# Row fetches of a graph-and-attention kernel divided over two more queues, and the cell's output kept in PSUM

## The reference, cut to what matters

```python
x = x + gnn(layernorm(x), edge_index)      # x is 6250 x 256
x = x + slice_attention(layernorm(x))      # 8 heads, 64 slices

agg = segment_sum(x[src], dst)             # 106,250 edges, sorted by dst
h = relu(agg @ W_rel + b_rel + x @ W_root) # 512 wide
i, f, g, o = split(h @ W_ih.T + b_ih + b_hh)
c = sigmoid(i) * tanh(g)
h_lstm = sigmoid(o) * tanh(c)
y = h_lstm @ W_fc + b_fc
```

## Time and profile before

| what | value |
|---|---|
| three runs | 1239.16, 1241.82, 1243.43 us; median 1241.82 |
| the profiled execution | 1240.34 us, of which 1238.5 us is the span from first to last instruction |
| PE busy | 1116.1 us (90%), granted clock 0.994 |
| DVE, POOL, ACT busy | 831.8 (67%), 805.3 (65%), 627.2 us (51%) |
| 22 turns from 184.60 to 1084.19 us | 899.59 us, 40.89 us each |

### The profile page before, as it was taken

One profiled execution on the slowest core, in us unless ns is written; L12 is line 12 of the kernel. 1 busy time (PEld: TensorE's weight loads), 2 busy tenths in 40 slices (PEclk: granted clock), 3 DMA queues, 4 the chain that ended last, 5 costly groups with the idle time before them and its releaser, 6 DMA issues. The chain is left out here.

```text
span 1238.5 us, 30254 instructions
## 1 busy us (share of the span) xinstructions
PE 1116.1 (90%) x9821; PEld 967.1 (78%) x9821; DVE 831.8 (67%) x2560; ACT 627.2 (51%) x1257; POOL 805.3 (65%) x856
## 2 busy tenths in 40 slices
PE   1077799999999999999999999999999999999998
PEld 0046688878888888788888787888888878897798
DVE  7885476667666766676677756775767566746665
ACT  5872444554456454545554545455545454555332
POOL 5877777777777777777777777777777777400000
PEclk9998999999999999999999999999999999999999
DMA  8674444444454445444544444444444454313498
GB/s 313 225 268 119 125 130 136 147 142 136 129 148 142 141 124 150 140 140 123 150 149 138 121 148 150 137 121 150 147 136 122 150 149 137 97 44 116 129 336 290
DMA packets 92966, 188.74 MB, mean 152 GB/s; under 512 B 20914, under 2 KB 55591, under 8 KB 92821
## 3 DMA queue, kind: packets, MB, share of 16 engines
q0 software_dynamic: 39168, 107.01, 30.0%
q1 hardware_dynamic: 42794, 59.89, 14.8%
q10 hardware_dynamic: 10859, 20.05, 4.5%
HBM read 154.87 MB, written 32.00 MB: 151 GB/s over the span
## 5 line engine op out<-in xcount | busy, mean ns | idle before, releaser
L700 POOL DMA_INDIRECT ring<-table,sidx x798 | 763.5, 957 | 247.5 <-issue 242.7
L419 PE MATMUL ps<-h_h,wih_h 128*128 128x250 f32 x1200 | 338.8, 282 | 0.0
L420 PE MATMUL ps<-h_l,wih_h 128*128 128x250 f32 x1200 | 336.5, 280 | 0.0
L421 PE MATMUL ps<-h_h,wih_l 128*128 128x250 f32 x1200 | 336.5, 280 | 0.0
L419 PEld LDWEIGHTS ps<-h_h,wih_h 128*128 128x128 f32 x1200 | 230.1, 192 | 2.0 <-issue 0.8
L420 PEld LDWEIGHTS ps<-h_l,wih_h 128*128 128x128 f32 x1200 | 230.2, 192 | 1.1
L421 PEld LDWEIGHTS ps<-h_h,wih_l 128*128 128x128 f32 x1200 | 230.1, 192 | 0.0
L850 ACT ACTIVATE gate<-ps,bgate 128x250 f32<-128x250 f32 x300 | 124.2, 467 | 140.7 <-PE ps L421 139.7
L651 DVE TENSOR_SCALAR oneh<-iota,didx 128x64 f16<-128x64 f16 (+2 forms) x1179 | 183.1, 259 | 0.0
L1078 PE MATMUL ps<-ring,oneh 128*32 128x512 f16 x2280 | 151.0, 391 | 34.5 <-DMA ring<-table,sidx 31.9
L1078 PEld LDWEIGHTS ps<-ring,oneh 128*32 128x32 f16 x2280 | 59.5, 97 | 107.7 <-DMA ring<-table,sidx 46.4
(11 more groups left out here) (213 smaller groups left out, 2508.4 us busy)
## 6 DMA issues: line engine op xcount, KB each, us to landing
sp_ring<-table SPq DMA_DIRECT2D x1920, 1.0 KB
ring<-table,sidx POOLq DMA_INDIRECT x798
swt_d<-swt ACTq DMA_DIRECT2D x25, 500.0 KB
gate<-swt_d SPq DMA_DIRECT2D x19, 500.0 KB, 5.9
x_room<-in_x SPq DMA_DIRECT2D x12, 512.0 KB, 10.6
xn<-table SPq DMA_DIRECT2D x25, 224.0 KB
xin<-in_x SPq DMA_DIRECT2D x25, 224.0 KB
res<-xin SPq DMA_DIRECT2D x25, 224.0 KB
```

The costliest lines, as they stand in the source:

```text
L419: eng.matmul(dst, wh, xh, start=first, stop=False)
L420: eng.matmul(dst, wh, xl, start=False, stop=False)
L421: return eng.matmul(dst, wl, xh, start=False, stop=last)
L700: pool.indirect_dma_start(ring[:, j, :], None, table, bass.IndirectOffsetOnAxis(ap=idx, axis=0)).then_inc(done, 16)
```

## The change

1. The chunks that are fetched row by row come one in 33 instead of one in 52: 23 chunks instead of 15. POOL's list is 8 chunks shorter (790 instead of 798 from the table).
2. Of each such chunk SP fetches rows 0 to 77, with a register load for each 26, and ACT rows 78 to 127, with a register load for each 10. Before a new chunk both wait until the sums that read the slot's last chunk are through. ACT's rows stand between its other instructions: 49 in a turn, with five register loads. ACT also begins with 30 rows ahead of its first turn. ACT's loop over turns is written out.
3. `hf` is no longer an SBUF tile but the PSUM bank of the first half of the sums, for two column blocks at a time. So the first pair is rounded and its remainder taken before the third block is made, each pair's remainder is one instruction instead of two, and DVE adds the first half of the sums ahead of `hots` and of the first `cell_o`, since that bank must be free.

The core of the diff:

```diff
-    SP_FIRST, SP_STEP, SP_N, SP_SLOTS = 86, 52, 15, 3
+    SP_FIRST, SP_STEP, SP_N, SP_SLOTS = 86, 33, 23, 3
-    ROWS_FIRST, ROWS, LOADS = 96, (8, 16, 60), 32
+    ROWS_FIRST, ROWS, LOADS = 78, (6, 14, 60), 26
+    SP_ROWS = 3 * LOADS
+    ACT_ROWS = P - SP_ROWS
+    ACT_FIRST, ACT_LOADS = 30, 10
...
+        hf = ps[:, SUM_A, :].rearrange("p (m n) -> p m n", m=2)[:, :, 0:PW]
...
+            def load_rows():
+                r = loaded[0]
+                if r < last_row and r < row_at[0] + 2 * ACT_LOADS:
+                    k, q = r // ACT_ROWS, r % ACT_ROWS
+                    if q == 0:
+                        wait_slot(act, k)
+                    for i, start in enumerate(load_starts(act, k, SP_ROWS + q, ACT_LOADS)):
+                        starts[r + i] = start
+                    loaded[0] += ACT_LOADS
...
             def turn(t, odd, gather, gnn, ffn, ahead):
+                if t == 0:
+                    for _ in range(ACT_FIRST // ACT_LOADS):
+                        load_rows()
+                        fetch_rows(ACT_LOADS)
                 if gnn:
                     split_x(t - 1)
+                    for _ in range(1 if ffn else 2):
+                        load_rows()
+                        fetch_rows(10)
                     relu_h(t - 1, 0)
+                    fetch_rows(1)
...
                         act.activation(ps[0:WN, XA + e, :], ps[0:WN, XA + e, :], ACT.Exp).then_inc(lg_exp, 1)
+                        fetch_rows(1)
...
                 if gnn:
+                    high_hl(t - 1, 0)
                     tanh_c(t - 1, 2)
+                    fetch_rows(1)
...
-            with act.Fori(lo, hi, step) as t:
+            for t in range(lo, hi, step):
...
             def cell_o(p, f):
-                if f == 0:
-                    after(dve, y_mm, p)
+                if f == 2:
+                    dve.wait_ge(hl_lo, 2 * p + 1)
...
+                if gather:
+                    add_halves(t, 0)
                 if gather and gnn:
                     hots(dve, 2 * t + 1)
                 if gnn:
                     cell_c(t - 1, 0)
                     cell_o(t - 1, 0)
-                if gather:
-                    add_halves(t, 0)
...
                 if gnn:
+                    low_hl(t - 1, 0)
                     cell_o(t - 1, 2)
                     cell_c(t - 1, 3)
                     cell_o(t - 1, 3)
...
-                    low_hl(t - 1, 0)
                     low_hl(t - 1, 1)
```

More of the change, by code:

```diff
@@ L438, in out_count, with wait_slot, load_starts, fetch_row @@
             return 16 * (len(range(q, NCH + 1, TILES)) + (len(REST_PARTS) - 1 if q == NCH % TILES else 0))
+        rows8 = table.bitcast(U8).rearrange("n c -> (n c)")
+        row_bytes = 4 * C
+        def wait_slot(eng, k):
+            if k == 0:
+                eng.wait_ge(spi_done, 1)
+            if k >= SP_SLOTS:
+                b = last_reader(SP_CHUNKS[k - SP_SLOTS])
+                eng.wait_ge(sum_done[b % 2], b // 2 + 1)
+                eng.wait_ge(sum_done[(b - 1) % 2], (b - 1) // 2 + 1)
+        def load_starts(eng, k, q, n):
+            _, at = nc.values_load_multi_w_load_instructions(
+                sp_idx[k:k + 1, q:q + n], engines=[eng.engine], min_val=0, max_val=(N - 1) * row_bytes,
+                skip_runtime_bounds_check_because="the DMA checks its bounds")
+            return at
+        def fetch_row(eng, k, q, start):
+            to = sp_ring[q:q + 1, k % SP_SLOTS, :].bitcast(U8)
+            eng.dma_start(to, rows8[ds(start, row_bytes)].rearrange("(p c) -> p c", p=1)).then_inc(
+                sp_rows[k % SP_SLOTS], 16)
         @block.sync
@@ L517, in _ @@
             row_at = [0]
-            rows8 = table.bitcast(U8).rearrange("n c -> (n c)")
-            row_bytes = 4 * C
             def fetch_rows(n):
-                for r in range(row_at[0], min(row_at[0] + n, SP_N * P)):
-                    k, q = r // P, r % P
+                for r in range(row_at[0], min(row_at[0] + n, SP_N * SP_ROWS)):
+                    k, q = r // SP_ROWS, r % SP_ROWS
                     if q == 0:
[L526 to L531, removed]
-                    if q % LOADS == 0:
[L533 to L539, removed]
+                        wait_slot(sp, k)
+                    if q % LOADS == 0:
+                        starts[:] = load_starts(sp, k, q, LOADS)
+                    fetch_row(sp, k, q, starts[q % LOADS])
                 row_at[0] += n
@@ L890, in turn @@
                 if gnn:
-                    gates(t - 1, 0, 4)
+                    fetch_rows(3)
+                    gates(t - 1, 0, 2)
+                    load_rows()
+                    fetch_rows(2)
+                    gates(t - 1, 2, 4)
                     tanh_c(t - 1, 0)
+                    load_rows()
+                    fetch_rows(8)
                 if ffn:
@@ L901, in turn @@
                 if gnn:
-                    gates(t - 1, 4, 8)
+                    gates(t - 1, 4, 6)
+                    fetch_rows(1)
+                    gates(t - 1, 6, 8)
+                    fetch_rows(1)
                     tanh_c(t - 1, 1)
+                    fetch_rows(3)
                     gates(t - 1, 8, 10)
+                    load_rows()
+                    fetch_rows(3)
                 if ffn:
@@ L1622, in low_hl @@
                 dve.wait_ge(hl_hi, 2 * p + q + 1)
[L1623 to L1625 removed]
+                dve.tensor_tensor(hl_l[:, 2 * q:2 * q + 2, 0:PW], hf, hl_h[:, 2 * q:2 * q + 2, 0:PW].bitcast(F32),
+                                  ALU.subtract).then_inc(hl_lo, 1)
             count = [0]
```

32 lines of the change are left out of this document (25 added, 7 removed).

## The result

| | median us | range | against the kernel before on the same chip |
|---|---|---|---|
| before | 1242.32 | 1239.16 to 1243.43 (4 runs) | |
| changed | 1300.57 | 1299.64 to 1302.69 (4 runs) | 1.0477 (95%: 1.0455 to 1.0499) |

The change costs 4.8%; I had forecast 1235 us and a range of 1230 to 1246. (Of the queues only ACT's is new to fetching rows; POOL and SP did so before.) The profiled execution has a span of 1297.8 us against 1238.5. The 59.3 us sit almost wholly in the 22 turns from the third `at_h` on: these take 955.7 us instead of 899.6 (+56.1), the third `at_h` begins 3.5 us later, and what follows the last turn is 0.2 us shorter.

The account below looks back on a forecast made before the run. POOL's pace was taken as the limit, PE's turn only 0.93 us behind. Of 20.5 us to gain over 22 turns, 13.2 go to PE's longer turn, leaving -7.3 from 1240.34; with the median's offset 1235 us, range 1230 to 1246.

Parts of the forecast that it names:

- POOL's list: POOL's gathers up to the last one PE waits for: 9 fewer at 1.25 us, 11.3 us earlier while POOL stays the limit.
- A row: Issue of one row on ACT: 0.32 us, costing nothing behind a running instruction of 0.4 us or more.
- The load of ten: ACT's register load of ten addresses: taken as 0.97 us, between bounds of 0.49 and 2.13.
- my line: Straight line from a load of one register, 0.49 us, to one of 32, 2.13; it gives 0.97 for ten.
- my 0.99: Behind the store on ACT, a load and two rows make `at_h` 0.99 us late; alone this costs PE nothing.
- The path of my sum: ACT's load and ten rows ahead of the ReLUs make them late; PE waits for the normalised rows, 0.6 us a turn.
- my sum: PE's turn grows by 0.6 to 40.56 us and PE becomes the limit: -7.3 us, expected 1235; chance 0.38.
- The cell's output: Output in PSUM with its new order: ACT's last copies 0.60 us later, output layer 0 to 0.1 later.
- The first turn: ACT's 30 rows ahead of it make it some 5 us late, taken up by PE's 5.4 and 5.0 us gather waits.
- the floor of 600 ns: Skill's floor for a register load; as an estimate 0.6 us each, with the ReLUs on time, against a measured 486 ns.

Follow-up runs that it names:

- rows alone: Changed kernel with the cell's output back in SBUF and the old order on DVE and ACT; 1275.72 us, ratio 1.0298 to the kernel before.
- twelves: Changed kernel with 80 rows on SP by loads of twenty, 48 on ACT by twelve, all 16-byte starts, end-of-turn load dropped: ratio 0.9899; with output in SBUF, old order: 0.9914.
- aligned tens: Changed kernel with ACT's row addresses copied to a table where each group of ten starts on a multiple of 16 bytes; 1246.19 us, ratio 1.0021 to the kernel before.

## Why the prediction was wrong

- **POOL's list: right.** Its waits left the stretch, and 790 gathers at 957 ns are what I had named.
- **A row: right.** Rows hide under running instructions; with the loads gone the turn is 40.25 us.
- **The load of ten: the step that failed.** I took 0.97 us, "as the time grows with registers and ten is nearer one than 32". It measured 2.10 on the mean (241.4 / 115), and its real neighbours were not on my line: the price goes by the start as well as the count. I had bounded it at 2.13, priced that bound at +43, and left it outside the range. Even the bound was not one: 38 of the 115 loads were below it, the other 77 above. Aligning ACT's loads takes 49.8 of the 56.1 us of the 22 turns back.
- **What the loads do then: the path was wrong too.** In the turn shown, the `at_h` that I had 0.99 us late, 0.39 of it behind the store, is 3.0 late there alone. I had put my 0.99 at nothing, as PE is in the output layer until about 677. That held for it, with some 0.3 us to spare, but not for 3.0. PE waits for `xt_l` in 21 turns, 1.7 us in each, the largest of its waits. The path of my sum, late ReLUs and PE waiting for the normalised rows, shows in 9 of 21 turns only (11.9 us). The wait for the softmax weights grew from 14.3 to 20.2 us.
- **The clock: not in my sum.** I added PE's waits to a turn of busy PE at full clock. Here waits also went with stretches at half clock, and 12 of the 56 us are PE's longer busy time.
- **The cell's output: the delay right, its price not.** I had ACT at the store 0.60 us later, and the 6.95 us up to the store, against 6.26 in rows alone, bear that out. In my sum this delay is the 0.6 a turn (without it the ReLUs are some 0.1 late). At PE's sums and output layer I left 0 to 0.1; from the last token sum to the output layer PE takes 0.20 more (1.56 us instead of 1.36, medians). On the misaligned loads the order costs (955.66 - 931.76) / 22 = 1.09 a turn. On the aligned ones it costs 0.60, of which the third `at_h`, 5.2 us later without the order in the profiled executions, takes back 0.24. With twelves it costs nothing.
- **The first turn: half right.** The first `at_h` came 3.6 us later than before, and 5.4 later than with the loop written out alone, near my 5. PE's 10.4 us of waits for gathers in the two turns behind it are gone, as I had it. But 7.6 us for `xt_l` and 7.7 for DVE's `wxs_l` took their place, and the third `at_h` is still 3.5 us late. With aligned tens it is 2.0 early, and with these and the output in SBUF 3.2 late: what absorbs the delay stays open.

That the aligned tens with the output in SBUF take 892.62 / 22 = 40.57 us, where I had forecast 40.56, is luck: that kernel lacks the 0.60 and has loads that are 0.21 us dearer than mine. PE waits there for `xt_l` (10.0 us in the 22 turns) and hardly for the normalised rows (1.2). The aligned tens with all of the change are the nearer test: my sum with 0.21 more for each of the two loads gives 40.56 + 0.42 = 40.98, and they take 41.17. So the price of the load was the larger error; its way to PE was wrong as well.

The Trainium skill states two things on such a price. "DMA: Bandwidth & Descriptors", section on latency and other measured facts, has the floor of 600 ns that I weighed. "Runtime: NRT & Kernel Launch", section on instruction fetch mechanics, has about 200 ns for each register even in bulk, said there of loads from HBM around a launch, which I did not weigh. The runs, whose loads read SBUF, agree with the latter off the 16-byte grid (5.62 / 26 = 0.22 us, 6.79 / 32 = 0.21, 2.38 / 10 = 0.24) and differ from it on the grid (2.13 / 32 = 0.07).

## What to carry to other kernels

When a step's price has wide bounds and one end of them flips the sign, the range must hold that end; nearness in count is no argument until the rows show what else the price depends on. Load addresses into registers in groups of four from 16-byte starts, and choose the split of the rows by that (80 and 48, not 78 and 50). A move that gains on a kernel with one limit may cost on a kernel with another: after a change moves the limit to an engine, go through that engine's queue again for each wait that was harmless. When a change makes PE wait, look at its granted clock too, not only at the sum of its waits.

## What the runs showed of the hardware

- A register load's price by start and count, medians: one 0.49 us (on SP); on a multiple of 16 bytes twelve 0.97, ten 1.18, twenty 1.48, 26 2.06, 32 2.13; 8 bytes off it ten 2.38, 26 5.62, 32 6.79. On the grid this reads as one price for each group of four and one for each address left over (3, 4, 5, 8 and 8 pieces); starts 4 or 12 bytes off were not run.
- A load right behind the 500 KB store on the same queue took longer: a median of 3.23 us against 2.38 off the grid (12 loads), and 2.37 and 2.11 against 1.18 on it (9 loads of the changed kernel, 21 of the aligned tens). Why was not tested.
- In the changed kernel's 22 turns the granted clock fell to 0.50 eight times, 27 us in all, each time with or right after a wait of PE for `xt_l` of 1.8 to 2.4 us; three such waits had no fall with them. In the 22 turns of the kernel before it never fell.
